# Cross-attention and quantised FFN: the softmax turned by DMA instead of TensorE, in a deeper pipeline

## The chip, the cores and the metric

The kernel runs on one core of a Trainium2 chip. The metric is the device time of one execution in microseconds (us). Engines: PE is TensorE's matmul part and PEld its weight load, DVE is VectorE, ACT ScalarE, POOL GpSimd, SP SyncE (which issues all DMAs here).

## The reference

With x of 8 x 128 x 512 and a context of the same shape, all in float32:

```
xn  = layernorm(x);  h = concat(ctx, xn)         # 256 keys per batch
q   = xn @ Wq        # 32 heads of 128, in 4 groups of 8
k,v = h @ Wk, h @ Wv # 4 heads of 128, one per group
x   = x + softmax(q k^T / sqrt(128)) v @ Wo
x   = x + FFN(layernorm(x))
```

The FFN is gate and up (512 to 1376), a sigmoid gate and down, with weights quantised to 4 bits in blocks of 32 and activations quantised to 16 bits over the minimum and maximum of the whole tensor, so each of its stages waits for an extreme over everything.

## The kernel before, in words

Every float32 operand of a matmul is split into two fp16 parts, upper (`hi`, ScalarE, line 522) and lower (`lo`, VectorE, line 698, the rest after the upper part is taken away), and a product is three matmuls. K and V of all four groups are made first (to about 102 us). Then comes the attention, as 64 steps: group g of 4, and within it k = 0 to 15, each step for one batch (k // 2) and four of the group's eight heads (k % 2). The first three groups are a loop whose body is one group; the fourth is written out. FFN follows from about 700 us.

One step on TensorE (`step`, line 411): the scores of the next step (line 339, 12 matmuls of 256 columns), the softmax of this step turned with keys onto partitions (`transpose_p`, line 356, eight float32 transposes of 128x128 into two PSUM banks), a weight unit's transposes (`transpose_w`, line 395), one head of the queries four steps ahead, the head output (`head_out`, line 366, 6 matmuls of 512 columns), another head of queries, and the projection with Wo (`project`, line 376, 12 matmuls of 512 columns), whose last four wait for the lower part of the head output.

Each engine has its own written-out order for a step, and engines meet by semaphores only. ScalarE (line 588): upper parts of the two banks of the turned softmax, the four exponentials of the next step (`exps`, line 575), the unit's upper part, the head output's upper part, the queries' upper part, a part of Wo for the next group. VectorE (line 848): maxima of the next step, lower parts of the two banks, the unit's scales, reciprocals, the unit's lower part, the head output's lower part, the unit's rounding, the queries' lower part, lower parts of Wo and Wq, and in odd steps the addition to y. GpSimd (line 1093): upper parts of Wq, `unit_normalise`, `normalise` (the softmax of the next step), `unit_dequantise`.

A weight unit is a 128x512 tile of the FFN's weights. 33 of them are prepared in steps 0 to 10 of the three groups of the loop: loaded (`load_unit`), scaled and normalised, rounded, dequantised, turned by TensorE in the next step, split, and stored to a scratch tensor in HBM (`store_unit`). Wo of the next group is loaded and split in steps 1 to 8 and Wq in steps 9 to 12. All loads and stores go through SyncE's queue in the order in which they are written, each behind its wait; `load_wq` (line 201) waits until the slice that held its buffer is lowered. In the last four steps of the last group (`late_step`) there are no queries left, and x is normalised and turned for the FFN instead.

Of the kernel before, what the change touches and what calls it, by code (L numbers as in the profile page):

```python
# [18 lines left out]
P = 128  # L19
B, T, H = 8, 128, 512  # L20
TOK = B * T
HC = H // P
# [22 lines left out]
LATE = 12  # L45
# [11 lines left out]
def build(nc, x, ctx_t, wq, wk, wv, wo, w_units, w_ready, out):  # L57
    stack = ExitStack()
    with stack:
# [22 lines left out]
        p_s = f32(160, 1024).rearrange("p (h t) -> p h t", h=4)  # L82
        pt_s = f16(164, 2048).rearrange("p (r c t) -> p r c t", r=2, c=2)
# [13 lines left out]
        wgu = f16(0, 2 * FT * 1024).rearrange("p (u r n) -> p u r n", u=2 * FT, r=2)  # L97
        xln2 = f32(48, 4096).rearrange("p (b h) -> p b h", b=B)
        x2t = f32(80, 4096).rearrange("p (c t) -> p c t", c=HC)
        xq = f16(44, 8192).rearrange("p (r c t) -> p r c t", r=2, c=HC)  # L100
# [12 lines left out]
        psums = small("psums", [P, 4])  # L113
        rsum = small("rsum", [P, 4])
# [19 lines left out]
        banks = [stack.enter_context(nc.psum_tensor(f"bank{i}", [P, 512], F32)) for i in range(8)]  # L134
        SC, TR, OB, YB, QB, WB = 0, 2, 4, 5, 6, 7
# [22 lines left out]
        tr_mm, pt_hi, tr_free = sem("tr_mm"), sem("pt_hi"), sem("tr_free")  # L158
# [34 lines left out]
        def _(sp):  # L193
# [37 lines left out]
            for s in w_stored:  # L231
                sp.sem_inc(s, 16)
            with sp.Fori(0, NG - 1) as g:
# [17 lines left out]
            sp.wait_ge(pv_mm, 2 * QUADS + 1)  # L251
            wgu_flat = wgu.rearrange("p u r n -> p u (r n)")
            sp.dma_start(wgu_flat[:, 0:FT], ready_d[:, 0:FT]).then_inc(wg_loaded, 16)
            sp.dma_start(wgu_flat[:, FT:2 * FT], ready_d[:, FT:2 * FT]).then_inc(wu_loaded, 16)
# [9 lines left out]
        def _(pe):  # L264
# [74 lines left out]
            def scores(g, k, extra=0):  # L339
# [5 lines left out]
                for j in range(2):  # L345
                    if not (isinstance(g, int) and g == 0 and k == 0):
                        pe.wait_ge(exp_out, 4 * t - 2 + 2 * j)
                    for hh in (2 * j, 2 * j + 1):
                        h = hq * 4 + hh
                        o = banks[SC + j][:, (hh % 2) * 256:(hh % 2) * 256 + 256].rearrange("p (u t) -> p u t", u=2)  # L350
# [3 lines left out]
                    mm.then_inc(sc_mm, 1)  # L354

            def transpose_p(g, k):

                t = g * QUADS + k
                pe.wait_ge(norm_out, t + 1)
                for c in range(2):  # L360
                    pe.wait_ge(tr_free, 2 * t + c + 1)
                    for hh in range(4):
                        mm = nc.tensor.transpose(banks[TR + c][:, hh * P:(hh + 1) * P], p_s[:, hh, c * P:(c + 1) * P], ident[:, :])  # L363
                    mm.then_inc(tr_mm, 1)

            def head_out(g, k):

                t, b = g * QUADS + k, k // 2
                for c in range(2):
                    pe.wait_ge(tr_free, 2 * t + c + 3)  # L370
                    for n, (i, r) in enumerate(((0, 0), (0, 1), (1, 0))):
                        mm = nc.tensor.matmul(banks[OB][:, :], kv[:, g + 1, 2 + i, (c * B + b) * P:(c * B + b + 1) * P],  # L372
                                              pt_s[:, r, c, :], start=c == 0 and n == 0, stop=c == 1 and n == 2)
# [37 lines left out]
            def step(g, k):  # L411

                t = g * QUADS + k
# [4 lines left out]
                pair = (k // 4 + 1) % 4  # L418
                if k >= 12:
                    pe.wait_ge(wq_lo, g * GH + GH + 2 * (k % 4) + 2)  # L420
                pe.wait_ge(q_lo, t + 4)
                q_head(QB, 2 * (k % 4), pair, k)
                head_out(g, k)
# [754 lines left out]
```

## Time and profile before

| | |
|---|---|
| time of three runs | 943.86, 944.35, 945.84 us; median 944.35 |
| profiled execution | span 944.5 us, 16272 instructions (no other time is listed for it) |
| PE, PEld busy | 861.5 us (91%), 539.1 us (57%) |
| DVE, ACT, POOL busy | 663.7 us (70%), 452.6 us (48%), 256.4 us (27%) |
| DMA | 52.14 MB in 39756 packets, 16.7% of 16 engines' span |
| mean granted TensorE clock | 0.960 of full speed |

Busy time of PE is modelled: matmuls are pipelined and the duration of one reaches into the next, so the length of a group is better read from the start of the next group than from its own duration. Idle time of an engine that is not the bottleneck costs nothing.

### The profile page before, as it was taken

What the parts mean: (1) busy time and instruction counts of PE and PEld (TensorE: products, weight loads), DVE (VectorE), ACT (ScalarE), POOL (GpSimd) and SP (SyncE); (2) the same over time, 40 slices, a digit from 0 to 9 for tenths busy, and PEclk for the clock granted to TensorE, in tenths of its full rate; (3) what the DMA queues carried; (4) which work ended last, traced back from release to release, by engine and by line L of the source; (5) the groups of instructions that cost most, each with busy time, mean ns of one, the idle gap of its engine ahead of it and who ended that gap; (6) DMA issues with size and microseconds to landing.
All of it is one profiled execution on the core that took longest, in us unless ns stands there. A gap on an engine that the chain in (4) does not pass through costs nothing. (4 is left out here: it accounts for less than half of the span.)

```text
span 944.5 us, 16272 instructions
## 1 busy us (share of the span) xinstructions
PE 861.5 (91%) x5390; PEld 539.1 (57%) x5390; DVE 663.7 (70%) x1333; ACT 452.6 (48%) x1029; POOL 256.4 (27%) x382
## 2 busy tenths in 40 slices
PE   9999999999899999989999999999868999900898
PEld 3444777767577776657766677767533444400343
DVE  5754588886478888558888656667647459989741
ACT  5344455645346554436554454454513029868630
POOL 0000245453235464224455322222210002203000
PEclk9999999999989999999999999999998999965799
DMA  8013022222012313002232620000030000000001
GB/s 289 1 56 111 20 84 90 90 68 90 3 57 80 111 45 112 23 25 77 92 101 75 210 74 1 2 1 1 1 123 1 1 0 1 1 0 0 12 33 45
DMA packets 39756, 52.14 MB, mean 55 GB/s; under 512 B 2432, under 2 KB 18816, under 8 KB 39680
## 3 DMA queue, kind: packets, MB, share of 16 engines
q1 hardware_dynamic: 39680, 51.13, 16.7%
q8 instruction: 48, 0.79, 0.4%
q14 instruction: 28, 0.23, 0.1%
HBM read 40.37 MB, written 10.75 MB: 54 GB/s over the span
## 5 line engine op out<-in xcount | busy, mean ns | idle before, releaser
L523 ACT ACTIVATE arena<-bank 128x512 f16<-128x512 f32 (+1 forms) x329 | 189.5, 599 | 342.8 <-PE bank L363 234.9
L698 DVE SCALAR_TENSOR_TENSOR arena<-bank,arena 128x512 f16<-128x512 f32 (+1 forms) x329 | 219.1, 686 | 87.8 <-ACT arena L523 87.7
L270 PE MATMUL bank<-arena 128*128 128x256 f16 (+2 forms) x1872 | 261.8, 292 | 0.0
L270 PEld LDWEIGHTS bank<-arena 128*128 128x128 f16 (+1 forms) x1872 | 183.8, 98 | 69.0
L1067 POOL TENSOR_SCALAR arena<-arena,rsum 128x256 f32<-128x256 f32 x256 | 135.2, 528 | 241.2 <-DVE rsum L792 223.5
L465 PE MATMUL bank<-arena 128*128 128x512 f16 x528 | 116.3, 384 | 8.9 <-DVE arena L698 8.9
L387 PE MATMUL bank<-arena 128*128 (+1 forms) x512 | 121.0, 379 | 0.7 <-ACT arena L523 0.7
L579 ACT ACTIVATE arena<-bank,nmax 128x256 f32<-128x256 f32 x256 | 118.1, 487 | 6.2 <-DVE nmax L788 6.2
L784 DVE TENSOR_REDUCE nraw<-bank 128x2 f32<-128x512 f32 x128 | 85.4, 689 | 36.1 <-PE bank L352 36.1
L352 PE MATMUL bank<-arena 128*128 (+1 forms) x768 | 97.4, 277 | 9.4 <-issue 7.2
L352 PEld LDWEIGHTS bank<-arena 128*128 128x128 f16 x768 | 75.8, 99 | 33.6 <-issue 11.2
L372 PE MATMUL bank<-arena 128*128 128x512 f16 x384 | 93.4, 379 | 1.7 <-DVE arena L698 1.6
L465 PEld LDWEIGHTS bank<-arena 128*128 128x128 f16 x528 | 52.1, 99 | 73.0 <-issue 12.0
L698 DVE SCALAR_TENSOR_TENSOR arena<-arena 128x512 f16<-128x512 f32 (+3 forms) x98 | 82.2, 850 | 9.0 <-ACT arena L523 8.8
L387 PEld LDWEIGHTS bank<-arena 128*128 128x128 f16 x512 | 50.0, 98 | 47.9 <-ACT arena L523 1.2
L363 PE MATMUL bank<-ident,arena 128*128 128x128 f32 x512 | 68.9, 279 | 5.7 <-POOL arena L1067 5.7
L1081 POOL TENSOR_TENSOR arena<-arena,winv 128x512 f32<-128x512 f32 x33 | 34.6, 1049 | 143.9 <-DVE winv L804 143.9
L627 ACT ACTIVATE arena<-arena,qc 128x1024 int32<-128x1024 f32 (+3 forms) x57 | 55.3, 999 | 26.9 <-DVE qc L930 26.9
L391 PE MATMUL bank<-arena 128*128 (+1 forms) x256 | 65.7, 379 | 0.0
L363 PEld LDWEIGHTS bank<-ident,arena 128*128 128x128 f32 x512 | 60.0, 144 | 8.4 <-POOL arena L1067 3.9
L523 ACT ACTIVATE arena<-arena 128x512 f32 (+3 forms) x74 | 51.1, 691 | 26.0 <-DVE arena L951 19.2
L297 PE MATMUL bank<-warm 128*128 128x512 f16 x50 | 16.0, 488 | 51.1 <-DVE worst L913 49.6
(91 smaller groups left out, 738.9 us busy)
## 6 DMA issues: line engine op xcount, KB each, us to landing
arena<-in_w_units SPq DMA_DIRECT2D x33, 256.0 KB, 2.8
w_ready<-arena SPq DMA_DIRECT2D x33, 256.0 KB, 2.1
arena<-w_ready SPq DMA_DIRECT2D x3, 2816.0 KB, 10.9
arena<-in_wq SPq DMA_DIRECT2D x32, 256.0 KB, 2.9
arena<-in_wo SPq DMA_DIRECT2D x32, 256.0 KB, 2.7
arena<-in_x SPq DMA_DIRECT2D x1, 2048.0 KB, 15.4
out<-arena SPq DMA_DIRECT2D x8, 256.0 KB, 2.0
arena<-in_wk SPq DMA_DIRECT2D x4, 256.0 KB, 5.2
```

The source lines that it names most:

```text
L270: last = nc.tensor.matmul(bank, a(i, c), b(j, c), start=start and c == 0 and n == 0, stop=stop and c == chunks - 1 and n == 2)
L352: mm = nc.tensor.matmul(o, q_s[:, buf, i, h, (b % 2) * P:(b % 2) * P + P], kv5[:, g + 1, r, :, b * P:(b + 1) * P], start=n == 0, stop=n == 2)
L363: mm = nc.tensor.transpose(banks[TR + c][:, hh * P:(hh + 1) * P], p_s[:, hh, c * P:(c + 1) * P], ident[:, :])
L372: mm = nc.tensor.matmul(banks[OB][:, :], kv[:, g + 1, 2 + i, (c * B + b) * P:(c * B + b + 1) * P], pt_s[:, r, c, :], start=c == 0 and n == ...
L387: nc.tensor.matmul(banks[YB][:, :], o_s[:, 0, hh * P:(hh + 1) * P], wo_s[:, par, r, hq * 4 + hh, :], start=hq == 0 and hh == 0 and r == 0, ...
L391: mm = nc.tensor.matmul(banks[YB][:, :], o_s[:, 1, hh * P:(hh + 1) * P], wo_s[:, par, 0, hq * 4 + hh, :], start=False, stop=hq == 1 and hh ...
L465: mm = nc.tensor.matmul(banks[t % 4][:, :], wgu[:, m * FT + t, i, c * P:(c + 1) * P], xq[:, j, c, bass.ds(th * 512, 512)], start=c == 0 an ...
L523: return nc.scalar.activation(dst, src, ACT.Copy, scale=scale)
L579: nc.scalar.activation(p_s[:, hh, :], banks[SC + hh // 2][:, (hh % 2) * 256:(hh % 2) * 256 + 256], ACT.Exp, bias=nmax[:, hh:hh + 1], scale ...
L698: return nc.vector.scalar_tensor_tensor(out=dst, in0=src, scalar=scale, in1=part, op0=ALU.mult, op1=ALU.subtract)
L784: nc.vector.tensor_reduce(nraw[:, 2 * j:2 * j + 2], banks[SC + j][:, :].rearrange("p (h t) -> p h t", h=2), AX.X, ALU.max, negate=True).th ...
L1067: last = nc.gpsimd.tensor_scalar(p_s[:, hh, :], p_s[:, hh, :], rsum[:, hh:hh + 1], P_SCALE, ALU.mult, ALU.mult)
```

## The change

The eight transposes of a step's softmax leave TensorE, and with them the two PSUM banks and the evictions by ScalarE and VectorE. Instead ScalarE takes the fp16 upper part of the normalised softmax from SBUF (`p_upper`), GpSimd the lower part (`p_lower`), and one transposing DMA on SyncE's queue (`turn_p`) turns both parts, 128 partitions x 2048 fp16, into the tile that the head output reads; p, its fp16 parts and the turned tile have two buffers each. The two free banks hold a second set of scores: scores now run two steps ahead of the head output instead of one, the queries six instead of four, and the projection of a step comes one step later (except in step 15). Wq of the next group is loaded and split in steps 7 to 10 instead of 9 to 12, its first two loads in step 5. The unit's lower part moves to the front of VectorE's step. The maxima of four heads are one instruction each. In the last group the FFN's gate and up weights are loaded in 22 pieces between the transposing DMAs rather than in two.

```
SyncE
+            def turn_p(t, k):
+                sp.wait_ge(p_lo, t + 1)
+                sp.sem_inc(sp_passed, 1)
+                sp.dma_start_transpose(pt_s[:, k % 2].rearrange("p r c (h t) -> p (r c h) t", h=4),
+                                       p_16[:, k % 2].rearrange("p r n -> p (r n)")).then_inc(pt_loaded[k % 2], 16)
                     if k < GH:
                         load_wo(g + 1, k)
-                    if k == 7:
+                    if k == 5:
                         load_wq(g + 1, 0)
                         load_wq(g + 1, 1)
-                    if 9 <= k <= 11:
-                        load_wq(g + 1, 2 * (k - 8))
-                        load_wq(g + 1, 2 * (k - 8) + 1)
+                    if 7 <= k <= 9:
+                        load_wq(g + 1, 2 * (k - 6))
+                        load_wq(g + 1, 2 * (k - 6) + 1)
+                    turn_p(g * QUADS + k + 1, k + 1)
                     if 1 <= k <= FT:
                         store_unit(g, k - 1)
                     if k < FT - 1:
                         load_unit(g, k + 1)
TensorE, step
-                scores(*((g, k + 1) if k < QUADS - 1 else (g + 1, 0)))
-                transpose_p(g, k)
+                scores(*((g, k + AHEAD) if k < QUADS - AHEAD else (g + 1, k + AHEAD - QUADS)))
                 if not last(g) and 1 <= k <= FT:
                     transpose_w(g, k - 1)
-                q_head(QB, 2 * (k % 4), pair, k)
-                head_out(g, k)
-                q_head(QB, 2 * (k % 4) + 1, pair, k).then_inc(q_mm, 1)
-                project(g, k)
+                if k >= 1:
+                    project(g, k - 1)
...
+                if k == QUADS - 1:
+                    head_out(g, k)
+                q_head(QB, 2 * (q % 4), (q // 4) % 4, k)
+                if k < QUADS - 1:
+                    head_out(g, k)
+                q_head(QB, 2 * (q % 4) + 1, (q // 4) % 4, k).then_inc(q_mm, 1)
+                if k == QUADS - 1:
+                    project(g, k)
ScalarE, step
-                for c in range(2):
-                    act.wait_ge(tr_mm, 2 * t + c + 1)
-                    hi(pt_s[:, 0, c, :], banks[TR + c][:, :], 1.0).then_inc(pt_hi, 1)
                 if not (final and k == QUADS - 1):
-                    exps(t + 1)
+                    p_upper(t + 1, k + 1)
                 if not final and 1 <= k <= FT:
                     unit_hi(g, k - 1)
+                if not (final and k >= QUADS - AHEAD):
+                    exps(t + AHEAD, k + AHEAD)
...
+                if not final and 1 <= k <= GH:
+                    wo_part(g + 1, k - 1)
                 act.wait_ge(pv_mm, t + 1)
                 act.wait_ge(wo_mm, t + 1)
                 hi(o_s[:, 0, :], banks[OB][:, :], HEAD_OUT).then_inc(o_hi, 1)
                 if not late:
-                    q_part(t + 4, (k // 4 + 1) % 2, 2 * (k % 4), QB)
+                    q_part(t + Q_AHEAD, (q // 4) % 2, 2 * (q % 4), QB)
VectorE, step
-                if not (final and k == QUADS - 1):
-                    maxima(t + 1)
-                for c in range(2):
-                    dve.wait_ge(pt_hi, 2 * t + c + 1)
-                    lo(pt_s[:, 1, c, :], banks[TR + c][:, :], pt_s[:, 0, c, :], 1.0).then_inc(tr_free, 1)
+                if not final and 1 <= k <= FT:
+                    unit_lo(g, k - 1)
+                if not (final and k >= QUADS - AHEAD):
+                    maxima(t + AHEAD, k + AHEAD)
                 if not final and k < FT:
                     unit_scales(g, k)
...
                 dve.wait_ge(o_hi, t + 1)
...
                 if not final and k < FT:
                     unit_round(g, k)
GpSimd, step
+                if not (final and k == QUADS - 1):
+                    p_lower(t + 1, k + 1)
-                if not final and 9 <= k <= 12:
+                if not final and 7 <= k <= 10:
...
                 if not final and k < FT:
                     unit_normalise(g, k)
-                if not (final and k == QUADS - 1):
-                    normalise(t + 1)
+                if not (final and k >= QUADS - AHEAD):
+                    normalise(t + AHEAD, k + AHEAD)
                 if not final and k < FT:
                     unit_dequantise(g, k)
```

## Rows read from the trace of the kernel before

**Rows 1.** Timeline of TensorE, a step without a unit: start us, us, engine, line, instructions.
```profile
646.62 1.47 PE L352 MATMUL bank<-arena 128*128 128x256 f16 x12
...
647.93 1.04 PE L363 MATMUL bank<-ident,arena 128*128 128x128 f32 x8
...
648.80 1.47 PE L270 MATMUL bank<-arena 128*128 128x256 f16 x12
...
650.12 1.46 PE L372 MATMUL bank<-arena 128*128 128x512 f16 x6
...
651.41 1.47 PE L270 MATMUL bank<-arena 128*128 128x256 f16 x12
...
652.72 1.89 PE L387 MATMUL bank<-arena 128*128 128x512 f16 x8
...
655.31 1.47 PE L352 MATMUL bank<-arena 128*128 128x256 f16 x12
```

**Rows 2.** Timeline of a step with a weight unit.
```profile
424.85 0.60 PE L400 MATMUL bank<-ident,arena 128*128 128x128 f32 x4
...
425.28 1.47 PE L270 MATMUL bank<-arena 128*128 128x256 f16 x12
...
429.33 0.42 DVE L810 TENSOR_SCALAR arena<-arena 128x512 f32<-128x512 f32 x1
...
429.78 0.59 DVE L812 TENSOR_SCALAR arena<-arena 128x512 f32<-128x512 f32 x1
```

**Rows 3.** Timeline from step 9 of the first group into step 12.
```profile
199.94 2.37 DVE L698 SCALAR_TENSOR_TENSOR arena<-arena 128x512 f16<-128x512 f32 x2
...
200.85 1.47 PE L352 MATMUL bank<-arena 128*128 x12
201.08 1.83 SPq L206 DMA_DIRECT2D arena<-in_wq  x2
...
221.16 1.04 PE L352 MATMUL bank<-arena 128*128 x8
```

**Rows 4.** Groups of GpSimd's instructions: busy us, mean ns | idle before.
```profile
L1067 POOL TENSOR_SCALAR arena<-arena,rsum 128x256 f32<-128x256 f32 x256 | 135.2, 528 | 241.2 <-DVE rsum L792 223.5
L1087 POOL TENSOR_TENSOR arena<-arena,wscale 128x512 f32<-128x512 f32 x33 | 43.1, 1306 | 2.6
L1081 POOL TENSOR_TENSOR arena<-arena,winv 128x512 f32<-128x512 f32 x33 | 34.6, 1049 | 143.9 <-DVE winv L804 143.9
```

**Rows 5.** Timeline of the last head output and the end of the attention.
```profile
690.85 1.46 PE L372 MATMUL bank<-arena 128*128 128x512 f16 x6
692.35 0.60 ACT L523 ACTIVATE arena<-bank 128x512 f16<-128x512 f32 x1 [3.29 <-PE bank L372]
692.98 0.69 DVE L698 SCALAR_TENSOR_TENSOR arena<-bank,arena 128x512 f16<-128x512 f32 x1 [2.56 <-ACT arena L523]
...
695.39 2.47 PEld L297 LDWEIGHTS bank<-warm 128*128 128x128 f16 x12
```

**Rows 6.** Timeline of the maxima and exponentials of one step.
```profile
400.78 1.35 DVE L784 TENSOR_REDUCE nraw<-bank 128x2 f32<-128x512 f32 x2 [1.92 <-PE bank L352]
...
402.04 0.29 DVE L788 TENSOR_SCALAR nmax<-nraw 128x2 f32<-128x2 f32 x2
...
402.84 0.48 ACT L579 ACTIVATE arena<-bank,nmax 128x256 f32<-128x256 f32 x1
...
404.91 0.60 ACT L523 ACTIVATE arena<-bank 128x512 f16<-128x512 f32 x1
```

**Rows 7.** DMA issues: count, KB each, median us from issue to landing.
```profile
arena<-in_w_units SPq DMA_DIRECT2D x33, 256.0 KB, 2.8
...
arena<-w_ready SPq DMA_DIRECT2D x3, 2816.0 KB, 10.9
```

**Rows 8.** Timeline of TensorE at the start of the attention.
```profile
103.34 2.78 PE L270 MATMUL bank<-arena 128*128 128x256 f16 x24
...
113.53 1.46 PE L372 MATMUL bank<-arena 128*128 128x512 f16 x6
```

More of the change, by code:

```diff
@@ L44 @@
 KB = 256
-LATE = 12
+AHEAD = 2
+Q_AHEAD = 6
+LATE = QUADS - Q_AHEAD
 P_ACT = range(5, 10)
@@ L112, in build @@
         nmax = small("nmax", [P, 4])
[L113 to L114 removed]
+        psums = small("psums", [P, 2, 4])
+        rsum = small("rsum", [P, 2, 4])
         mhalf = small("mhalf", [P, B])
@@ L353, in scores, with head_out @@
                                                   kv5[:, g + 1, r, :, b * P:(b + 1) * P], start=n == 0, stop=n == 2)
[L354 to L359, printed above, removed]
+                mm.then_inc(sc_mm, 1)
+            def head_out(g, k):
+                b = k // 2
+                pe.wait_ge(pt_loaded[k % 2], 16 * (g * (QUADS // 2) + k // 2 + 1))
                 for c in range(2):
[L361 to L368, printed above, removed]
-                for c in range(2):
-                    pe.wait_ge(tr_free, 2 * t + c + 3)
                     for n, (i, r) in enumerate(((0, 0), (0, 1), (1, 0))):
                         mm = nc.tensor.matmul(banks[OB][:, :], kv[:, g + 1, 2 + i, (c * B + b) * P:(c * B + b + 1) * P],
-                                              pt_s[:, r, c, :], start=c == 0 and n == 0, stop=c == 1 and n == 2)
+                                              pt_s[:, k % 2, r, c, :], start=c == 0 and n == 0, stop=c == 1 and n == 2)
                 mm.then_inc(pv_mm, 1)
@@ L441, in _ @@
                     scores(0, 0)
-                pe.wait_ge(wq_lo, 2 * f + 2)
+                if f == 5:
+                    scores(0, 1)
+                if f < 4:
+                    pe.wait_ge(wq_lo, 2 * f + 2)
                 if f == 0:
@@ L604, in step @@
                 if not late:
-                    q_part(t + 4, (k // 4 + 1) % 2, 2 * (k % 4), QB)
-                if not final and 1 <= k <= GH:
-                    wo_part(g + 1, k - 1)
+                    q_part(t + Q_AHEAD, (q // 4) % 2, 2 * (q % 4), QB)
             def copy_x2(b):
@@ L612, in copy_x2 @@
                                      ACT.Copy, scale=1.0).then_inc(x2_copied, 1)
-            for f in range(4):
+            for f in range(Q_AHEAD):
                 if f == 3:
-                    exps(0)
-                q_part(f, 0, 2 * f, QB + f % 2)
+                    exps(0, 0, first=True)
+                if f == 5:
+                    exps(1, 1, first=True)
+                    p_upper(0, 0)
+                q_part(f, f // 4, 2 * (f % 4), QB + f % 2)
             with act.Fori(0, NG - 1) as g:
@@ L884, in step @@
                     ln2_apply(k // 2 - 1)
-                if k % 2 and not late:
+                if k == QUADS - 1:
                     add_y(k // 2, t)
-            for f in range(4):
+            for f in range(Q_AHEAD):
                 if f == 3:
-                    maxima(0)
-                    reciprocals(0)
-                q_part(f, 0, 2 * f, QB + f % 2)
+                    maxima(0, 0)
+                    reciprocals(0, 0)
+                if f == 5:
+                    maxima(1, 1)
+                    reciprocals(1, 1)
+                q_part(f, f // 4, 2 * (f % 4), QB + f % 2)
             with dve.Fori(0, NG - 1) as g:
@@ L1103, in step @@
                     unit_normalise(g, k)
-                if not (final and k == QUADS - 1):
-                    normalise(t + 1)
+                if not (final and k >= QUADS - AHEAD):
+                    normalise(t + AHEAD, k + AHEAD)
                 if not final and k < FT:
@@ L1112, in _ @@
             pool.sem_inc(w_dq, 1)
-            normalise(0)
+            normalise(0, 0)
+            normalise(1, 1)
+            p_lower(0, 0)
             with pool.Fori(0, NG - 1) as g:
```

140 lines of the change are left out of this document (75 added, 65 removed).

## The prediction

> **What bounds the kernel now.** I read the page's shares first (TensorE 91% busy, VectorE 70%, ScalarE 48%, GpSimd 27%), then the timeline of one step of the last head group, then of a step that also prepares a weight unit, then what stands at the loop's edges. The reader is to see in the first timeline that the starts of TensorE's groups follow one another with no idle bracket [rows 1]: scores at 646.62, transposes of the softmax 647.93, half of the queries 648.80, head output 650.12, the other half 651.41, projection 652.72, next scores 655.31. So one step takes 8.69 us, and its parts are 1.31 (scores), 0.87 (the eight transposes), 1.32 and 1.31 (queries), 1.29 (head output), 2.59 (projection). In steps 1 to 11 of the three groups of the loop the transposes of a weight unit add 0.43 [rows 2], together 9.12. TensorE is the bound, and every other engine has slack, in this order of the work. Two steps in each group are over it: from 200.85 to 221.16 two of them take 20.31 instead of 18.25 [rows 3], 2.06 us; they are the ones in which SyncE issues loads of Wq behind waits for VectorE.
>
> **The change, part by part.** *Removed:* 512 transposes, 0.87 us in each of 64 steps, 55.7 us in all if TensorE stays the bound; ScalarE loses two evictions and VectorE two, GpSimd gains one subtraction.
>
> *The steps without a weight unit* (12 to 15 and 0 of three groups, 0 to 9 of the last: 25) get the whole of it, -21.8 us. From scores two steps ahead to the head output there are then 2 x 7.82 + 1.31 + 2.59 + 1.32 = 20.9 us, and the chain (scores 1.31, maxima 1.5, exponentials 2.1, normalise four times 0.53, upper part 1.1 or two evictions less a start, lower part 2.1 to 2.6 or twice the 128x512 of [rows 4], with some 2 us of queueing) takes 12 to 13 before the transfer, which therefore has about 8 us.
>
> *The steps with a weight unit* don't. The unit's chain crosses the head output: GpSimd's dequantise(k) waits for VectorE's rounding(k), which is queued behind the lower part of the head output(k). TensorE's transposes of unit k come right behind the scores of step k+1. Before, the head output followed those transposes after 0.43 + 1.32 us; now the projection(k-1) lies between as well, 2.59 more, and the 0.87 of softmax transposes that stood ahead of the unit's are gone. The cycle from one unit's transposes to the next: 0.43 + projection 2.59 + queries 1.32, head output to its eviction 1.50 and on to the subtraction 0.63 [rows 5], subtraction 0.69, roundings 0.45 + 0.59 [rows 2], dequantise 1.05 (as its twin) to its own mean of 1.31 [rows 4], semaphores 0.1: 9.35 to 9.61. A second path takes as long in steps 2 to 8: the unit's upper part is now ahead of the exponentials on ScalarE and its lower part ahead of the maxima on VectorE: 0.43 + 0.21 + 0.63 + 0.65, maximum to its scaling 1.26, scaling 0.2, exponentials 2.07 [rows 6], the Wo part 0.6, then again 0.63 + 0.69 + 0.45 + 0.59 + 1.05 to 1.31 + 0.1: 9.6 to 9.9. TensorE's own work is 8.25. I take 9.6, so these steps are not 0.87 faster but 0.48 slower: ten intervals in each of three groups, +14.4. The first link (step 0 to 1) is short on TensorE, 5.2 us of work, and the same chain from head output to dequantise holds it 1.4 us each time: +4.2.
>
> *The transfer.* No row shows a transposing DMA. From 256 KB in 2.8 us and 2816 KB in 10.9 [rows 7] a plain copy of the step's 512 KB would take 2.8 + 8.1/10 = 3.6. Bounds by the rows: 2.8 and 10.9. I take L = 4.5, near the 3.6, since it handles 2-byte elements. The Trainium skill (DMA: Bandwidth & Descriptors, Latency and other measured facts) gives a transposing DMA 261 GB/s with a non-contiguous middle dimension, and a DMA about 2 us of fixed cost (Anatomy of one DMA, for GpSimd's queue); by that 512 KB would take 4.0, and the sum would be 5 us lower; no row here shows it.
>
> *The queue it stands in.* SyncE issues the transposes in order with the loads. In steps 7, 8 and 9 it first issues two Wq loads, each waiting until VectorE has lowered the slice that held its buffer, the last thing VectorE does in that step. Before, the pair of step 9 ended 1.46 us into the next step and the second load was out at 2.06 [rows 3]; nothing but loads was behind it. Now the query's subtraction that precedes it starts some 2.9 us later (the projection no longer follows the queries, the rounding comes later) and in steps 7 and 8 a Wo part stands ahead too (0.75): the transfer can start 4.6 to 5.7 us into the next step, whose head output TensorE reaches at 7.0 with the 1.35 that it waits for the unit. The stall is L - 2.0, L - 2.0 and L - 2.9: 2.5 + 2.5 + 1.6 = 6.6 us per group, +19.8. The unit's load, queued behind the transfer, is late by a similar amount, on a parallel path, and I add nothing. The 2.06 of before is contained: -6.2. Bounds: nothing at L = 2.0, +54 at L = 8.
>
> *Start.* Two more query pairs and one more score stand ahead of the loop, and GpSimd lowers step 0's softmax only behind normalise(1). From the second scores' end at 109.9 (two pairs of 2.62 from 103.34, scores 1.31; 103.34 is where the query pair behind the first scores begins): query evictions and maxima 111.6, exponentials 113.7, reciprocal and normalise 116.1, lower part 118.4, transfer 122.9, where head output 0 began at 113.53 before; both starts in [rows 8]: +9.4. *End.* From step 10 (646.62) to the last projection (695.39 [rows 5]) took 48.8. Now TensorE's work there is 31.5 (4 scores, 7 transposes of x, 6 head outputs, 6 projections), but steps this short run at the pace of maxima, exponentials, normalise, root and the layer norm behind them on VectorE, some 6.7 on average for four steps, and the last head output waits for its transfer: 44, so -4.8. The stages behind keep their length; the weights of the FFN are loaded in time (22 loads of 256 KB over 11 steps of 7.8 us).
>
> Sum: -21.8 + 14.4 + 4.2 + 19.8 - 6.2 + 9.4 - 4.8 = +15.0. The profiled span is 944.5, the median of the runs 944.35; no time of that execution is given apart from its span, and the two agree to 0.02%. Prediction 959.5 us. *At nothing:* ScalarE's upper part (1.1) takes the place of two evictions (1.1) and VectorE loses 1.3 per step, so neither becomes the bound by its sum; GpSimd comes to 2.4 + 2.1 + 1.05 + 1.3 = 6.9 us per unit step, 8.1 with two Wq parts, under 9.6, and if that cover went (contention on its reads) each 0.3 us on dequantise is 9 us.
>
> **Rivals.** *A, faster: the unit's chain doesn't bind and the transfer is short.* If L is 2.8 or less, as the 256 KB rows, the holds of steps 7 to 9 cost at most 1.6 per group, and if dequantise also came before its turn on TensorE, the 33 unit steps would gain 0.87 each: -0.87 x 58 - 6.2 + 4.8 + 7.7 - 4.8, about 895. For it: TensorE is 91% busy and the transposes are real work. Against: the two paths above are chains of measured durations, 1.3 us over TensorE's own. It decides at 8.25 us for the cycle. *B, short transfer, chain binds:* L about 2.5 takes 20 off the holds and the start: 939; with the cycle at its low end 9.35, 932. *C, slower still: the transfer is 7 to 9 us,* hidden in plain steps, but each us costs 10 over the three groups and the start: 984 to 1004. *D, the transfer is longer than a step can hide (over 9.3):* then every step waits, and where the transfers of SyncE's queue follow one another their length becomes the period: at 12 us 64 x 12 for 64 x 8.6, some 220 more, 1160. A figure of the Trainium skill speaks for this: VectorE: DVE Perf Modes, The three transpose paths, has 1309 ns for one 128x128 block of 2-byte elements by DMA; sixteen in turn would be 21 us a step, and by that the kernel would take some 1,700 us; no row here shows it, and it stands within D.
>
> **How the numbers follow.** Forecast (L 3.3 to 6.5, cycle 9.35 to 9.9) 0.52, own range 945 to 985; A 0.12; B 0.12; C 0.14; D 0.10. The range of 8 in 10 leaves out most of A and D: 925 to 1005. A measurement of this kernel tells 0.2% (1.9 us) from no change: faster than that 0.24 (A, most of B, a sliver of the forecast), within it 0.04, slower 0.72.
>
> **What would show it.** In the trace after: no softmax transposes on TensorE; scores 7.8 us apart in steps 12 to 15 and in the last group's first ten (right), 9.6 in unit steps with TensorE waiting for GpSimd's dequantise ahead of the unit's transposes (at 8.3 that step falls, and A holds); head output waiting for the transfer in steps 8, 9 and 10 alone (if in all steps, D; if nowhere, B); the transfer from issue to landing 4.5 us; head output 0 at about 123. The prediction is wrong if the transfer's length is far off, or if another queue than SyncE's carries the delay.

## The result and the profile after

The changed kernel takes 998.72 us (median of 4 runs, 995.4 to 1002.6) against 944.75 for the kernel before in the same comparison: ratio 1.0574, 95% interval 1.0536 to 1.0611. It is slower, as forecast, but by 54 us and not by 15. The time lies inside the range of 925 to 1005, and outside the forecast's own 945 to 985. The profiled execution has a span of 997.8 us, with a mean granted TensorE clock of 0.938 of full speed (0.960 before).

First the page of the kernel after: busy time by engine, and the group of the head outputs (busy us, mean ns | idle before it and its releaser).

```profile
PE 830.4 (83%) x4878; PEld 487.6 (49%) x4878; DVE 611.6 (61%) x1077; ACT 456.2 (46%) x965; POOL 392.7 (39%) x446
...
L380 PE MATMUL bank<-arena 128*128 128x512 f16 x384 | 100.8, 402 | 34.1 <-DMA arena<-arena 34.1
```

TensorE lost 31 us of busy time although the 512 transposes are gone (55.7 by their share of a step), because parts of its work now run at the lower clock (the same 384 matmuls of the head outputs are 100.8 us busy against 93.4 before); and the span grew by 53. The head outputs now have 34.1 us of idle time before them, ended by a DMA; 5.7 of it stands before the first one. What TensorE waits for is in the view of the waits (engine, line, waited for: us in total, times, longest), kernel after, from 113 to 700 us:

```profile
PE bank L408 <- POOL arena L1114: 53.8, 33, 5.0
PE bank L380 <- DMA arena<-arena: 33.1, 9, 5.7
```

L408 is a weight unit's transposes, L1114 GpSimd's dequantise, L380 the head output, and the DMA is the new transfer. I compare the kernels by intervals from the start of one head output to the next (the 64 starts of L380 after, of L372 before), all in us. Interval 7 is the one from head output 7 of a group to head output 8, and so on:

| | before | after | difference | predicted |
|---|---|---|---|---|
| first head output | 113.53 | 122.54 | +9.0 | +9.4 |
| plain interval, last group | 8.69 | 7.82 | -0.87 | -0.87 |
| unit interval, steps 1 to 6 | 9.1 | 9.5 to 9.8 | +0.4 to +0.7 | 9.6 |
| first link, per group | | | +1.9, +1.1, +1.6 | +1.4 |
| intervals 7 to 10, per group | 38.6, 38.8, 38.4 | 57.7, 62.5, 60.3 | +64.9 in all | +19.4 in all |
| last 15 intervals | 127.7 | 115.3 | -12.4 | |
| start of the last group's step 10 to last projection | 48.8 | 46.9 | -1.9 | -4.8 |

The sum: +9.0 at the start, the three groups of the loop +17.1, +19.2, +21.7, the last one -12.4, the rest -1.4: +53.2, the difference of the spans up to rounding (997.8 - 944.5 = 53.3). The four intervals 7 to 10 hold 64.9 of it, 45.5 more than predicted; everything else together came out at -11.6 where -4.4 was forecast (mostly the two edges inside the loop, see the smaller misses).

A plain step of the last group on TensorE, timeline of the kernel after (start us, us, engine, line, instructions), against [rows 1]: head output, queries, scores, projection, no transposes, no idle bracket, 7.81 from head output to head output.

```profile
645.90 1.46 PE L380 MATMUL bank<-arena 128*128 128x512 f16 x6
647.19 1.47 PE L288 MATMUL bank<-arena 128*128 128x256 f16 x12
648.50 1.47 PE L370 MATMUL bank<-arena 128*128 128x256 f16 x12
649.81 1.89 PE L395 MATMUL bank<-arena 128*128 128x512 f16 x8
...
653.71 1.46 PE L380 MATMUL bank<-arena 128*128 128x512 f16 x6
```

A unit step of the kernel after, against [rows 2]. The bracket behind a row is the idle time before it and what ended it.

```profile
143.15 1.46 PE L380 MATMUL bank<-arena 128*128 128x512 f16 x6
...
144.04 0.64 ACT L536 ACTIVATE arena<-arena 128x512 f32 x1
...
144.64 0.60 ACT L536 ACTIVATE arena<-bank 128x512 f16<-128x512 f32 x1
...
145.27 0.69 DVE L721 SCALAR_TENSOR_TENSOR arena<-bank,arena 128x512 f16<-128x512 f32 x1 [0.90 <-ACT arena L536]
...
146.51 0.58 DVE L833 TENSOR_SCALAR arena<-arena 128x512 f32<-128x512 f32 x1
...
147.18 1.05 POOL L1114 TENSOR_TENSOR arena<-arena,wscale 128x512 f32<-128x512 f32 x1 [0.36 <-DVE arena L833]
...
148.28 0.66 PE L408 MATMUL bank<-ident,arena 128*128 128x128 f32 x4 [1.05 <-POOL arena L1114]
```

The chain from head output to dequantise is the one of the forecast, and TensorE waits 1.05 for its end. The head output's eviction begins at 144.64, which is both the end of the head output and the end of ScalarE's preceding work (the Wo part from 144.04), so the two predicted paths meet there.

Steps 7 and 8 of the first group of the kernel after, against [rows 3]; DMA_DIRECT2D rows are loads and stores on SyncE's queue, x2 the pair of Wq.

```profile
191.16 1.46 PE L380 MATMUL bank<-arena 128*128 128x512 f16 x6
...
193.76 1.47 PE L370 MATMUL bank<-arena 128*128 x12
...
195.66 4.29 DVE L721 SCALAR_TENSOR_TENSOR arena<-arena 128x512 f32 x3
...
196.23 2.57 POOL L1094 TENSOR_TENSOR arena<-arena 128x1024 f16<-128x1024 f32 x1
...
199.57 1.01 SPq L210 DMA_DIRECT2D arena<-in_wq  x2
200.78 3.08 SPq L242 DMA_TRANSPOSE arena<-arena  x1
...
204.81 0.35 SPq L227 DMA_DIRECT2D arena<-in_w_units  x1
205.71 2.52 PE L380 MATMUL bank<-arena 128*128 128x512 f16 x6 [4.82 <-DMA arena<-arena]
207.42 0.69 DVE L820 TENSOR_REDUCE amax<-arena 128x16 f32<-128x512 f32 x1 [5.53 <-DMA arena<-in_w_units]
213.19 1.36 POOL L1114 TENSOR_TENSOR arena<-arena,wscale 128x512 f32<-128x512 f32 x1
214.61 0.66 PE L408 MATMUL bank<-ident,arena 128*128 128x128 f32 x4 [3.14 <-POOL arena L1114]
```

Read it downward. VectorE lowers a part of Wo and the pair of Wq (L721, three in 4.29 us) while GpSimd makes the softmax's lower part (L1094). Each of SyncE's two loads goes out behind the lower part of the slice that held its buffer, and only then the transfer, 7.0 us after the scores of the step (193.76 to 200.78). The head output waits for it. The unit's load is behind the transfer in the same queue, VectorE stands 5.53 us before its scales, and so the dequantise is late and TensorE waits once more. TensorE's 128x512 head output takes 2.52 us there and 1.46 at full clock.

### The profile page after: what moved, and what is told of

It reads as the page before. It is cut to its first block and busy times, and to the rows that moved or that the text cites. A ratio compares the mean times of both kernels' runs of the same rounds, so it can differ in the third digit from the quotient of the medians.

```text
span 997.8 us, 14844 instructions
## 1 busy us (share of the span) xinstructions
PE 830.4 (83%) x4878; PEld 487.6 (49%) x4878; DVE 611.6 (61%) x1077; ACT 456.2 (46%) x965; POOL 392.7 (39%) x446
## 5 line engine op out<-in xcount | busy, mean ns | idle before, releaser
L721 DVE SCALAR_TENSOR_TENSOR arena<-bank,arena 128x512 f16<-128x512 f32 (+1 forms) x201 | 137.0, 686 | 144.0 <-ACT arena L536 143.3
L536 ACT ACTIVATE arena<-bank 128x512 f16<-128x512 f32 (+1 forms) x201 | 119.0, 598 | 196.6 <-PE bank L288 97.8
L1094 POOL TENSOR_TENSOR arena<-arena 128x1024 f16<-128x1024 f32 x64 | 147.3, 2302 | 37.9 <-ACT arena L536 37.5
L536 ACT ACTIVATE arena<-arena 128x1024 f16<-128x1024 f32 (+5 forms) x138 | 119.1, 863 | 73.8 <-POOL arena L1087 47.8
L395 PE MATMUL bank<-arena 128*128 (+1 forms) x512 | 128.4, 396 | 2.1 <-ACT arena L536 2.1
L380 PE MATMUL bank<-arena 128*128 128x512 f16 x384 | 100.8, 402 | 34.1 <-DMA arena<-arena 34.1
L478 PE MATMUL bank<-arena 128*128 128x512 f16 x528 | 115.4, 382 | 8.8 <-DVE arena L721 8.8
L721 DVE SCALAR_TENSOR_TENSOR arena<-arena 128x512 f16<-128x512 f32 (+3 forms) x98 | 96.6, 1002 | 9.7 <-ACT arena L536 9.5
L370 PE MATMUL bank<-arena 128*128 (+1 forms) x768 | 96.5, 277 | 3.6 <-issue 3.6
L806 DVE TENSOR_REDUCE nraw<-bank 128x4 f32<-128x1024 f32 x64 | 77.9, 1217 | 7.0 <-PE bank L370 7.0
L380 PEld LDWEIGHTS bank<-arena 128*128 (+1 forms) x384 | 37.9, 101 | 74.1 <-issue 31.4
L1108 POOL TENSOR_TENSOR arena<-arena,winv 128x512 f32<-128x512 f32 x33 | 34.6, 1049 | 100.1 <-DVE winv L825 100.1
L650 ACT ACTIVATE arena<-arena,qc 128x1024 int32<-128x1024 f32 (+3 forms) x57 | 55.3, 999 | 27.2 <-DVE qc L950 27.2
L408 PE MATMUL bank<-ident,arena 128*128 128x128 f32 x132 | 22.6, 296 | 53.8 <-POOL arena L1114 53.8
L399 PE MATMUL bank<-arena 128*128 (+1 forms) x256 | 67.2, 386 | 0.0
```

The source lines that it names most:

```text
L370: mm = nc.tensor.matmul(o, q_s[:, buf, i, h, (b % 2) * P:(b % 2) * P + P], kv5[:, g + 1, r, :, b * P:(b + 1) * P], start=n == 0, stop=n == 2)
L395: nc.tensor.matmul(banks[YB][:, :], o_s[:, 0, hh * P:(hh + 1) * P], wo_s[:, par, r, hq * 4 + hh, :], start=hq == 0 and hh == 0 and r == 0, ...
L399: mm = nc.tensor.matmul(banks[YB][:, :], o_s[:, 1, hh * P:(hh + 1) * P], wo_s[:, par, 0, hq * 4 + hh, :], start=False, stop=hq == 1 and hh ...
L478: mm = nc.tensor.matmul(banks[t % 4][:, :], wgu[:, m * FT + t, i, c * P:(c + 1) * P], xq[:, j, c, bass.ds(th * 512, 512)], start=c == 0 an ...
L536: return nc.scalar.activation(dst, src, ACT.Copy, scale=scale)
L721: return nc.vector.scalar_tensor_tensor(out=dst, in0=src, scalar=scale, in1=part, op0=ALU.mult, op1=ALU.subtract)
```

## The experiments

All ratios are to the kernel before, of runs on the same chip (median of before 944.8 to 947.0). "Sum of 7 to 10" is the sum of those four intervals for the three groups; before it is 38.6, 38.8, 38.4, after 57.7, 62.5, 60.3.

**The order of SyncE's queue.** Three kernels move the issues of one loop step and nothing else. T is the theory that the late transfer holds these steps, U that the late load of the unit is enough by itself.

x1_turn_first: the transfer ahead of Wq's waits, the unit's load still behind them.

```
                     if k < GH:
                         load_wo(g + 1, k)
+                    turn_p(g * QUADS + k + 1, k + 1)
                     if k == 5:
...
-                    turn_p(g * QUADS + k + 1, k + 1)
```

> The changed kernel with the transposing DMA of a step issued ahead of the Wq loads of steps 7 to 9, and not behind them; the unit's store and load stay behind them. Theory T (what holds steps 7 to 10 is the transfer standing in SyncE's queue behind waits for VectorE): the head output's waits of 4.8, 1.6 and 1.6 us go, and with the first the fall of the clock behind it; the sum of steps 7 to 10 falls from 58 to about 45 us a group, the kernel from 998.7 to about 960. Rival U (the unit's load standing there is enough by itself): TensorE waits as long at the unit's transposes instead, about 990.

Measured: 983.14 us, ratio 1.0388 (1.0354 to 1.0421); sum of 7 to 10: 55.8, 55.0, 55.3. T's 960 is missed by far, and U's 990 is nearer.

x2_unit_first: the unit's store and load ahead of Wq's waits, the transfer still behind them.

```
+                    if 1 <= k <= FT:
+                        store_unit(g, k - 1)
+                    if k < FT - 1:
+                        load_unit(g, k + 1)
                     if k == 5:
```

> The changed kernel with the unit's store and load issued ahead of the Wq loads, the transposing DMA behind them. Theory T: little is won, 985 to 995, the head output waits 5 us in step 8 and the same afterwards. Rival U: the unit's transposes are on time, about 965 to 975.

Measured: 987.88 us, ratio 1.0433 (1.0403 to 1.0463); sum of 7 to 10: 57.1, 56.3, 56.6. Here T's 985 to 995 holds and U's 965 to 975 doesn't.

x3_wq_last: Wq's loads, with their waits, behind the transfer, the store and the unit's load.

```
(conditions and arguments left out)
+                    turn_p(...); store_unit(g, k - 1); load_unit(g, k + 1)
                     if k == 5:
...
                     if 7 <= k <= 9:
                         load_wq(g + 1, 2 * (k - 6))
                         load_wq(g + 1, 2 * (k - 6) + 1)
-                    turn_p(...); store_unit(g, k - 1); load_unit(g, k + 1)
```

> The changed kernel with the transposing DMA and the unit's store and load all ahead of the Wq loads. Both T and U: no wait of the head output for the transfer in the loop, the unit's transposes held only by their chain of 9.5 us and by the chain of the Wq slices through two buffers (load, upper, lower, 11.5 us for a pair): steps 7 to 10 at 9.5, 11, 11 and 10, 935 to 955. If neither queue place matters (rival V: VectorE and GpSimd are the bound in these steps through contention) it stays over 985.

Measured: 966.93 us (960.55 to 968.96), ratio 1.0221 (1.0187 to 1.0256); sum of 7 to 10: 49.9, 44.3, 49.0. That is 12 us above the 955 that both theories allowed. The waits of the three, in the order x1, x2, x3, each from 113 to 700 us:

```profile
PE bank L408 <- POOL arena L1114: 76.0, 33, 7.8
PE bank L380 <- DMA arena<-arena: 6.2, 2, 5.7
```

```profile
PE bank L380 <- DMA arena<-arena: 50.1, 10, 5.7
PE bank L408 <- POOL arena L1114: 28.7, 25, 2.2
```

```profile
PE bank L408 <- POOL arena L1114: 56.9, 33, 5.8
PE bank L380 <- DMA arena<-arena: 6.7, 3, 5.7
```

Moving only the transfer takes the waits for it away (33.1 to 6.2, of which 5.7 stand before the first head output in both) and gives most back as waits for the unit (53.8 to 76.0); moving only the unit's load does the reverse. Over before, the steps 7 to 10 cost 64.9 us with both issues late, 50.3 with the unit's load alone late (x1), 54.2 with the transfer alone late (x2), and 27.4 with neither (x3). So standing behind Wq's waits costs 37 us of these steps (64.9 - 27.4), and each of the two late issues is enough for 23 to 27 of them. The profile of x3 is of its fastest run, 6.4 us below its median; by the medians the new order is worth 32 us of the kernel's time. What is left in x3 is mostly another chain. Its timeline shows it:

```profile
201.91 0.62 POOL L1129 TENSOR_SCALAR arena<-arena 128x512 f16<-128x512 f32 x1 [3.95 <-DMA arena<-in_wq]
...
203.81 1.05 POOL L1108 TENSOR_TENSOR arena<-arena,winv 128x512 f32<-128x512 f32 x1
...
208.31 1.36 POOL L1114 TENSOR_TENSOR arena<-arena,wscale 128x512 f32<-128x512 f32 x1
...
209.73 1.11 PE L408 MATMUL bank<-ident,arena 128*128 128x128 f32 x4 [5.78 <-POOL arena L1114]
```

GpSimd waits at the head of its step for a Wq slice (L1129), 3.95 us; Wq has two buffers, so a pair can be loaded only when the pair before has been lowered, late in VectorE's step (here the lower parts end at 198.51 and 199.11 and the loads go out at 198.73 and 199.36). The unit's normalise (L1108) and dequantise are queued behind. The next step's transfer still goes out behind these loads, at 199.94, but its head output begins only at 216.4 and doesn't wait for it.

**The unit's cycle.** x4_unit_late puts the unit's transposes behind the projection and both evictions later; x5_late_pe does the TensorE part alone, x6_late_ev the evictions alone.

```
TensorE
                 scores(...)
-                if not last(g) and 1 <= k <= FT:
-                    transpose_w(g, k - 1)
                 if k >= 1:
                     project(g, k - 1)
+                if not last(g) and 1 <= k <= FT:
+                    transpose_w(g, k - 1)
ScalarE: unit_hi(g, k - 1) from ahead of exps to behind them
VectorE: unit_lo(g, k - 1) from ahead of maxima to behind reciprocals
```

> The changed kernel with the unit's transposes behind the projection on TensorE, its upper part behind the exponentials on ScalarE and its lower part behind the reciprocals on VectorE. Theory C (unit steps of 9.54 us are held by the two chains through the head output and through the exponentials): steps 1 to 6 at 8.25, steps 7 to 10 as before or worse, 970 to 985. Rival (contention of GpSimd's two-input subtraction is the hold): unchanged 9.5, about 998.

Measured: 965.4 us, ratio 1.0191 (1.0153 to 1.0229). That is 5 us below the 970 to 985 of the expectation. In steps 1 to 6 the intervals are 8.25 to 8.8. In its timeline the first units' transposes are 8.25 apart, TensorE's own work, and wait for nothing:

```profile
138.67 0.60 PE L408 MATMUL bank<-ident,arena 128*128 128x128 f32 x4
...
146.92 0.60 PE L408 MATMUL bank<-ident,arena 128*128 128x128 f32 x4
```

Steps 7 to 10 lose only 8.6 us in all (57.1, 58.0, 57.0), and nearly all of the waiting is now at the head output:

```profile
PE bank L380 <- DMA arena<-arena: 57.0, 12, 7.5
...
PE bank L408 <- POOL arena L1114: 0.5, 2, 0.3
```

> The changed kernel with only the unit's transposes moved behind the projection on TensorE. Theory C2 (two chains of equal length, one through the head output, one through the unit's upper and lower part ahead of exponentials and maxima): steps 2 to 6 stay at 9.4 to 9.6, the kernel within 5 us of 998. Rival C1 (only the chain through the head output holds): 8.25 to 8.8 as with both edits, 966 to 975.

Measured: 988.17 us (two runs), ratio 1.0439 (1.0373 to 1.0505). The two runs are 993.12 and 983.23, and their median is 5 us below the lowest that C2 allowed. Steps 2 to 6 stay at 9.5 to 9.8, as C2 has it; the first link falls to 8.2 in two of the three groups.

> The changed kernel with only the unit's evictions moved behind the exponentials (ScalarE) and the reciprocals (VectorE). Theory C2: steps 2 to 6 stay at 9.2 to 9.5, within 8 us of 998. Rival C3 (only the chain through the evictions holds): 8.25 to 8.8, 966 to 975.

Measured: 991.04 us (two runs), ratio 1.0470 (1.0433 to 1.0507). Steps 1 to 6 at 9.2; sum of 7 to 10: 58.5, 60.4, 60.0.

x4 gains 36 us, the two halves 13 and 10, with intervals of some 6 and 4 us either way. Each half alone leaves one of the two paths standing; only together do the steps come to 8.25 to 8.8. That the halves moved the whole at all is in part the first link in x5 and the last 0.3 to 0.4 of each step in x6.

**The clock.** x7_warm takes no wait away: it puts matmuls on a spare tile into TensorE's waits of the held steps, so that the engine does not stand idle. In the lines below, k of the first condition is the unit's number, so these matmuls stand in steps 9 to 11 (not 8 to 10, as the expectation has it), ahead of waits of 3.1, 4.3 and 3.5 us in the first group; the wait for `w_lo` moves ahead of them.

```
+                if 8 <= k <= 10:
+                    for _ in range(14):
+                        nc.tensor.matmul(banks[WB][:, :], warm[:, 0:P], warm[:, :], start=True, stop=True)
                 pe.wait_ge(w_dq, v + 2)
...
+                if not last(g) and k == 8:
+                    keep_warm(20)
```

> The changed kernel with matmuls on a tile of zeros where TensorE waits: 20 ahead of the head output in step 8 (4.3 us in a wait of 4.8) and 14 ahead of the unit's transposes in steps 8 to 10 (3.0 us in waits of 3 to 5; in step 8 the wait is 1.1, so 1.9 too long there). Theory K (part of the holds is the clock at half speed behind each long wait): the granted clock in the attention rises from 0.95 to over 0.98 and the kernel falls by 8 to 15 us, to 984 to 991. Rival (the slow matmuls stand in time that other engines need anyway): 996 to 1004.

Measured: 985.36 us, ratio 1.0398 (1.0367 to 1.0429); sum of 7 to 10: 55.8, 55.1, 54.8, which is 14.9 us less in all. In the kernel after, TensorE's rows in the second group show what it is:

```profile
400.18 1.89 PE L395 MATMUL bank<-arena 128*128 x8
...
414.89 1.12 PE L408 MATMUL bank<-ident,arena 128*128 128x128 f32 x4 [5.00 <-POOL arena L1114]
415.80 3.62 PE L395 MATMUL bank<-arena 128*128 x8
```

Behind a wait of 5 us, eight of the projection's matmuls take 3.62 us where they took 1.89, and four transposes 1.12 where they take 0.66 in an undisturbed unit step: the pace of the lower level, 1.2 GHz instead of 2.4, and the granted clock from 414.8 to 421 is 0.50. The windows of 113 to 700 (busy times, then the mean granted clock in the third column from the right) have 0.95 for the kernel after and 0.99 for x7:

```profile
113.00:700.00 587.00, 494.76 (x3223) 323.00 (x3222) 357.66 (x590) 269.39 (x689) 344.12 (x385) 0.95 0.49 111
```

```profile
113.00:700.00 587.00, 530.06 (x3497) 343.01 (x3495) 362.60 (x607) 277.47 (x710) 353.58 (x396) 0.99 0.49 115
```

**Together.** x8_both is x3 and x4.

> The changed kernel with the Wq loads last in SyncE's step and the unit's transposes and evictions late (the edits of the two runs that took 32 and 33 us off). If the holds of steps 7 to 10 and the chains of the unit steps are separate, the gains add: 930 to 940, below the kernel before (947). If they share their waits: 945 to 960.

Measured: 928.14 us, ratio 0.9806 (0.9783 to 0.9829). The two gains add (33.4 + 36.2 = 69.6 us off the kernel after, against 72.6). It is 1.9% faster than the kernel before. Sum of 7 to 10: 44.3, 45.8, 44.4.

x9_four gives Wq four buffers (the third and fourth are Wo's raw tile), with Wo's parts in steps 1 to 4 and 12 to 15, and lowers the first softmax ahead of the second's normalise at the start.

```
+            def load_four(g, j):
+                sp.dma_start(wq_four[:, j % 4], wq_d[:, :, bass.ds((g * GH + j) * D, D)]).then_inc(wq_turn[j % 4], 16)
...
-                if not final and 1 <= k <= GH:
-                    wo_part(g + 1, k - 1)
+                if not final and (1 <= k <= 4 or k >= 12):
+                    wo_part(g + 1, k - 1 if k <= 4 else k - 8)
```

> As the run with both edits, and the Wq slices go through four buffers (the two of Wo lent to them from step 5 to 10, Wo's parts in steps 1 to 4 and 12 to 15), so that the pair of step 8 is loaded before step 7 ends; the first lower part of the softmax is made before the second normalisation. Theory W (what is left in steps 8 to 10 is the chain load, upper, lower of a pair through two buffers): these steps fall to 8.5 to 9.5, 900 to 915. Rival (contention between VectorE's and GpSimd's two-input instructions): no more than 5 us below the run with both edits.

Measured: 917.29 us, ratio 0.9687 (0.9667 to 0.9708), 2 us above what was expected; each group's four intervals are 8.2, 10.5, 10.5, 10.5, and the one behind them grew to 9.5. The timeline of x9 names what still holds three steps of 8.3:

```profile
187.70 4.03 DVE L735 SCALAR_TENSOR_TENSOR arena<-arena 128x512 f16<-128x512 f32 x2
...
188.69 2.50 POOL L1108 TENSOR_TENSOR arena<-arena 128x1024 f16<-128x1024 f32 x1
...
191.65 1.21 DVE L820 TENSOR_REDUCE nraw<-bank 128x4 f32<-128x1024 f32 x1
...
196.22 1.02 PE L409 MATMUL bank<-arena 128*128 x4 [1.60 <-ACT arena L550]
```

The pair of Wq's lower parts takes 4.03 us beside GpSimd's subtraction (L1108 here), where one takes 0.69 alone, and the maxima (L820) are queued behind it; TensorE waits at the projection. x10_apart puts the pair behind the maxima of the next step, and the last two pairs of loads one step later.

```
                     maxima(t + AHEAD, k + AHEAD)
+                if not final and 8 <= k <= 11:
+                    for j in (2 * (k - 8), 2 * (k - 8) + 1):
+                        dve.wait_ge(wq_hi, g * GH + GH + j + 1)
+                        lo(wq_s[:, 1, :, j * D:(j + 1) * D], wq_four[:, j % 4], wq_s[:, 0, :, j * D:(j + 1) * D],
+                               W_SCALE).then_inc(wq_lo, 1)
```

> The run with four Wq buffers, with VectorE's lower parts of Wq moved from the end of steps 7 to 10, where they meet GpSimd's subtraction of the softmax, to behind the maxima of steps 8 to 11. Theory Q (two two-input instructions over SBUF, one on VectorE and one on GpSimd, wait for each other: a pair of lower parts takes 3.7 to 4.0 us beside the subtraction and 1.3 alone): steps 8 to 10 fall from 10.5 to 8.3 to 9, the kernel from 917 to 897 to 905. Rival (VectorE is simply full in these steps): within 4 us of 917.

Measured: 904.10 us (903.15 to 905.80), ratio 0.9551 (0.9522 to 0.9580): the fastest kernel here, 4.5% below the kernel before. Sum of 7 to 10: 36.7 in each group (8.3, 9.6, 9.4, 9.4), now below the kernel before, and the interval behind them is back at 7.8. The timeline of x10 shows that the pair still meets a subtraction and still takes long, but the maxima are ahead of it:

```profile
194.50 1.21 DVE L820 TENSOR_REDUCE nraw<-bank 128x4 f32<-128x1024 f32 x1
...
195.94 3.22 DVE L735 SCALAR_TENSOR_TENSOR arena<-arena 128x512 f16<-128x512 f32 x2
...
196.04 2.57 POOL L1108 TENSOR_TENSOR arena<-arena 128x1024 f16<-128x1024 f32 x1
```

**What in the subtraction slows VectorE.** x11_one_input puts two one-input GpSimd instructions in the place of the subtraction in the kernel after; the softmax's lower part is not computed in it.

```
-                nc.gpsimd.tensor_tensor(p_16[:, k % 2, 1, :], p_s[...], p_16[:, k % 2, 0, :], ALU.subtract).then_inc(p_lo, 1)
+                nc.gpsimd.tensor_scalar(p_16[:, k % 2, 1, :], p_s[...], 0.0, 1.0, ALU.mult, ALU.mult)
+                done = nc.gpsimd.tensor_scalar(p_s[:, k % 2], p_s[:, k % 2], 1.0, 1.0, ALU.mult, ALU.mult)
```

> The changed kernel with GpSimd's subtraction (one instruction with two inputs, 2.3 us) replaced by two instructions with one input each, of 1.08 us: the lower part of the softmax is left out (zeros). Theory Q: VectorE's lower parts of Wo and Wq beside it fall from 1.2 to 1.5 us each to 0.7 to 0.8; in steps 7 to 10 the transfer starts 1.5 to 2.5 us earlier, 5 to 8 us a group, 975 to 985. Rival (no part of contention): within 4 us of 998.

Measured: ratio 1.0464 (1.0405 to 1.0523), from runs of 986.85, 987.12 and 994.59 us; a fourth took 2216.35 us, which nothing here explains, and isn't in the ratio. That is some 10 us less than the kernel after, between the 975 to 985 of theory Q and the rival's 4 us. Timeline of x11 at the place of the kernel after's steps 7 and 8:

```profile
195.23 4.05 DVE L721 SCALAR_TENSOR_TENSOR arena<-arena 128x512 f32 x3
...
195.82 1.48 POOL L1095 TENSOR_SCALAR arena<-arena 128x1024 f16<-128x1024 f32 x1
...
197.27 1.47 POOL L1097 TENSOR_SCALAR arena<-arena 128x1024 f32<-128x1024 f32 x1
```

The second of these three lower parts by itself, in x11 and then in the kernel after, where it began while L1094 ran (196.23 to 198.80):

```profile
196.32 1.52 DVE L721 SCALAR_TENSOR_TENSOR arena<-arena 128x512 f16<-128x512 f32 x1
```

```profile
196.75 2.61 DVE L721 SCALAR_TENSOR_TENSOR arena<-arena 128x512 f16<-128x512 f32 x1
```

Three lower parts take 4.05 us, against 4.29, but the single ones differ: 1.16, 1.52, 1.52 here, and 1.16, 2.61, 0.68 in the kernel after. In both kernels each slow one ends 0.54 or 0.55 us behind the end of GpSimd's instruction. So VectorE's instruction waits until GpSimd's has ended, and what it loses is the rest of that one; in x11 a second pass is there to hold the third lower part too. GpSimd waits as well: the subtraction takes 2.13 us when no such instruction runs on VectorE (39 of 64) and 2.57 or 2.58 behind one (25). GpSimd's second input isn't needed for it. Two inputs in SBUF are needed on VectorE's side: 25 lower parts that read one input from PSUM kept their 0.69 us beside L1094.

## Why the prediction was wrong in size, point by point

*Right.* The sign and its reason: only the 25 plain steps gain. The plain interval came out at 7.82 as worked out (term -21.8), unit intervals at 9.5 to 9.8 for 9.6 (+14.4), the first link at +4.6 in all for +4.2, the start at +9.0 for +9.4, and the transfer at a median of 4.3 us from issue to landing for the assumed 4.5. The Trainium skill's 261 GB/s (DMA: Bandwidth & Descriptors, Latency and other measured facts), from which, with its 2 us of fixed cost (Anatomy of one DMA), I had estimated 4.0, agrees with the 4.3 to 0.3 us. Its 1309 ns for one 128x128 block (VectorE: DVE Perf Modes, The three transpose paths) doesn't add up over the sixteen blocks of one DMA (4.3 us and not 21); no run here turns one block alone. Rival D would have had every step wait, and the plain ones don't. x5 and x6 showed that both paths of the forecast bind at 9.2 to 9.5, and x4 that the cycle's place in the order, not its work, is the cause. That the time still lies within 925 to 1005 is luck: the upper end was there for a longer transfer, and the transfer wasn't longer.

*The step that failed* is the hold of steps 7 to 9: "The stall is L - 2.0, L - 2.0 and L - 2.9: 2.5 + 2.5 + 1.6 = 6.6 us per group, +19.8", with "The unit's load, queued behind the transfer, is late by a similar amount, on a parallel path, and I add nothing." By it the intervals 7 to 10 would be 12.1, 12.1, 11.2, 9.6. The means of the three groups are 14.6, 16.2, 14.5, 14.9, which is 2.5, 4.1, 3.3 and 5.3 more, 15.2 a group and 45.5 in all. What the runs put in its place:

- *The transfer starts later than I had it.* "The transfer can start 4.6 to 5.7 us into the next step": it is 7.0 in the rows above, from 193.76 (the step's scores) to 200.78. I took VectorE's lower parts at the price they have before, 2.37 us for the pair in [rows 3], where the dequantise runs beside it, and 0.75 for Wo's part, 3.1 together; the three took 4.29 us, of which one (2.61) had to wait for the end of the new subtraction. That is 1.2 of the 1.3 us over the latest start that I had allowed. The landing took 4.8 us here and not 4.5. The forecast had named contention as a risk, but on GpSimd's dequantise. x10 shows that taking these instructions from where they hold others is worth 13 us in a kernel whose queue is already mended.
- *The unit's load isn't free.* x2 takes it from behind the waits and gains 13.3 us; x1 alone, which frees the transfer, gains 17.6 and x3, which frees both, 33.4. So a late unit's load alone (x1) holds steps 7 to 10 nearly as long as a late transfer alone (x2), and reaches one step further: interval 10, for which I had nothing, takes 14.9 and falls to 10.2 in x2. "Parallel" was half right: with one late 50 and 54 us are lost, with both 65; over the 27 that x3 keeps that is 23, 27 and 37, so the two overlap without being hidden. But a parallel path as long as the first hides nothing once the first is mended.
- *Wq's own chain.* x3 keeps 27.4 us in these steps with neither of the two issues late. Four buffers, with Wo's parts moved away (x9), take 44.8 a group (x8's mean) to 39.7, where TensorE's own work is 4 x 8.25 = 33. The runs don't part the buffers from the other edits of x9.
- *The clock.* My sum had matmuls at full clock throughout. x7 gives 14.9 us back without taking a wait away. They lie inside the 45.5, not beside them, since they come with the waits, and x1 to x3 save part of them too; so the shares of the causes overlap and I do not split the 45 further.

*Smaller misses.* The end gained 1.9 and not 4.8: one of the late steps takes 11.4 us, where TensorE waits 3.7 us for ScalarE's copy of x and then runs at the lower clock. The loop's edge (intervals 14 and 15) gained 4.2 and 5.7 us in the first two groups and 1.8 in the third, of which I had counted 1.7 each. The forecast's upper bound for the hold, +54 at a transfer of 8 us, is +51 by its own formula (6.0 + 6.0 + 5.1 a group); nothing rests on it.

*Rivals.* A needed a cycle of 8.25 and didn't happen as the kernel stood, but x4 shows that it was within reach by order alone. B and C, on the transfer's length, fell with 4.3 us; the time came out in C's range (984 to 1004) by a mechanism that wasn't C's.

*Still open.* In x10 three steps of each group take 9.4 to 9.6 instead of 8.3; its waits name the dequantise (nine waits, 9.1 us in all, 113 to 660). Its trace has an order that would do it: in the first group a unit lands at 196.05, VectorE reaches its scales only behind the pair of Wq (195.94 to 199.16), and GpSimd its normalise at 200.74 and its dequantise at 204.39; no run moves the pair once more to test this. How the 37 us of standing behind the waits divide into delay and lower clock isn't told either. From 113 to 700 us the granted clock stood at 0.50 for 58 us in all in the kernel after and for 10 before, so by an estimate from these two the clock is at most 24 us (half of the difference) of what that stretch lost.

## What to carry to other kernels

When a transfer on which the critical engine waits joins an in-order queue, look for every wait written ahead of it and ahead of what is queued behind it: the cure here was to move the issues whose waits end late to the back of each step's list, and it had to be done for both users, since mending one only showed the other. When an order of work has two chains that close at the same engine, test them together: two edits worth about 10 and 13 us alone were worth 36 at once. And price an instruction by what will run beside it after the change, not by its row before.

## What the runs showed of the hardware

- VectorE's instruction with two inputs in SBUF and an instruction of GpSimd wait for each other. A 128x512 lower part takes 0.69 us alone, 2.61 beside GpSimd's 128x1024 subtraction (2.57) and 1.52 beside a one-input pass of 128x1024 (1.48), and ends 0.54 or 0.55 us behind it each time; with one of its inputs in PSUM it keeps 0.69. The other way round the subtraction goes from 2.13 to 2.57 us and the one-input pass from 1.05 to 1.48. The Trainium skill (GPSIMD Engine Reference, section 1. Specifications) says that the two engines share their SBUF interfaces, "contention with DVE instructions in a 2-port perf mode or with two SBUF inputs"; the rows agree as to the two SBUF inputs, and no run here shows the other case.
- One transposing DMA of 128 partitions x 2048 fp16 (512 KB) lands 4.3 us after its issue, median of 64 (4.2 to 6.2), and its instruction holds SyncE's queue for 1.3 to 3.6 us of that.
- Behind the wait of 5.00 us at 414.89 TensorE's matmuls ran at half pace, at a granted clock of 0.50 until 421, and feeding the engine matmuls on a spare tile in its waits (x7) kept the granted clock from 113 to 700 us at 0.99 instead of 0.95.
